# A graph attention and mixture-of-experts layer: accumulators kept in a 32-slot ring and stored once per node tile

## What is computed

```
h = einsum('nf,hfd->hnd', x, W);  a_s, a_d = h . att_src, h . att_dst       # per head
e = leaky_relu(a_s[:, src] + a_d[:, dst], 0.2)                              # edges and a self-loop of each node
for each head:
    m = segment_max(e, dst);  ex = exp(e - m[dst]);  den = segment_sum(ex, dst)
    out = segment_sum(h[src] * ex / den[dst], dst);  acc += softmax(gate)[head] * out
ln = layernorm(acc + bias + x);  result = ln @ Wo.T + bo
```

## Time and profile before

| | |
|---|---|
| median of 3 runs | 1814.36 us |
| lowest and highest | 1811.67, 1824.21 us |
| the profiled execution: time | 1812.91 us |
| its span | 1810.8 us |
| its mean granted TensorE clock | 0.824 of full speed |
| preparation | 0 to 190 us |
| edge phase: groups of products | 254 to 973 us |
| node stage, combine | 995 to 1118, 1118 to 1435 us |
| experts, final norm | 1450 to 1710, 1715 to 1808 us |
| PE, DVE, ACT, POOL busy, share of the span | 67, 58, 27, 37% |

### The profile page before, as it was taken

How to read it: one execution, slowest core, us unless ns; L and a number is a source line. 1 busy time by engine, 2 the same in 40 slices (tenths; PEclk the granted TensorE clock), 3 DMA queues, 4 the chain that set the end, 5 groups by cost and what they waited for, 6 DMA issues and landing times. The chain is left out here.

```text
span 1810.8 us, 29517 instructions
## 1 busy us (share of the span) xinstructions
PE 1220.3 (67%) x6148; PEld 994.7 (55%) x6149; DVE 1053.7 (58%) x3010; ACT 486.0 (27%) x1900; POOL 673.9 (37%) x781
## 2 busy tenths in 40 slices
PE   0795035666666776777784474999999179999800
PEld 0574023444444555555553353899998168999700
DVE  7656124556555666677785455678887433444357
ACT  0342011112221222222220233555553023333200
POOL 3000655656555454454300354244443201111164
PEclk9998556778887788897896656899999589999955
DMA  6015535566565656666644422334331395222155
GB/s 206 19 37 80 139 84 176 176 187 191 180 203 176 195 176 197 193 201 190 196 148 117 129 64 76 123 126 145 130 130 65 117 312 188 70 70 72 56 145 147
DMA packets 216712, 254.97 MB, mean 141 GB/s; under 512 B 53540, under 2 KB 190374, under 8 KB 212902
## 3 DMA queue, kind: packets, MB, share of 16 engines
q1 hardware_dynamic: 174262, 137.89, 24.9%
q0 software_dynamic: 30848, 103.40, 19.1%
q10 hardware_dynamic: 11504, 12.59, 2.1%
HBM read 138.88 MB, written 111.65 MB: 138 GB/s over the span
## 5 line engine op out<-in xcount | busy, mean ns | idle before, releaser
L683 POOL DMA_INDIRECT rows<-node_rows,srcT x391 | 381.7, 976 | 313.1 <-PE pO L947 179.7
L947 PE MATMUL pO<-rows,pw 128*128 x1184 | 381.1, 457 | 120.5 <-DVE pw L774 87.7
L790 DVE SCALAR_TENSOR_TENSOR acc<-acc,rsc,pO 128x257 f32<-128x257 f32 x592 | 282.4, 477 | 160.2 <-PE pO L947 74.0
L947 PEld LDWEIGHTS pO<-rows,pw 128*128 128x128 f32 x1184 | 243.0, 225 | 177.9 <-issue 143.2
L1355 PE MATMUL pW_<-W_again,aT 128*128 128x256 f32 x800 | 181.8, 381 | 0.0
L1355 PEld LDWEIGHTS pW_<-W_again,aT 128*128 128x128 f32 x800 | 148.9, 191 | 18.4
L1689 PEld LDWEIGHTS pHe<-xeT,w1e 128*128 128x128 f32 x1056 | 129.7, 194 | 9.9 <-DVE w1e L1727 6.6
L1689 PE MATMUL pHe<-xeT,w1e 128*128 128x128 f32 x1056 | 130.5, 277 | 5.7 <-DVE xeT L1707 4.8
L1745 POOL DMA_DIRECT2D ys_rows<-ye x66 | 35.7, 541 | 244.5 <-DVE ye L1737 244.5
L1698 PE MATMUL pYe<-w,hT 128*128 x528 | 125.3, 380 | 1.9 <-ACT hT L1668 1.1
L1668 ACT ACTIVATE hT<-pHe,b 128x128 f32<-128x128 f32 x264 | 75.5, 368 | 184.2 <-PE pHe L1689 172.7
(11 more groups left out here) (319 smaller groups left out, 2015.4 us busy)
## 6 DMA issues: line engine op xcount, KB each, us to landing
agg_rows<-acc SPq DMA_DIRECT2D x74, 1024.0 KB
w<-in_ffn_w SPq DMA_DIRECT2D x32, 512.0 KB, 5.6
xe<-xs_rows ACTq DMA_DIRECT2D x66, 128.0 KB, 2.0
ys_rows<-ye POOLq DMA_DIRECT2D x66, 128.0 KB, 2.0
rows<-node_rows,srcT POOLq DMA_INDIRECT x391
node_rows<-xna SPq DMA_DIRECT2D x25, 136.0 KB
xna<-in_x SPq DMA_DIRECT2D x5, 640.0 KB, 11.3
qs<-qT_y SPq DMA_DIRECT2D x25, 128.0 KB, 2.2
```

The lines of the kernel that those rows point to most:

```text
L683: pool.indirect_dma_start(rows[:, k % RING, :], None, node_rows[:, :], at_row(srcT[:, k:k + 1])).then_inc(s_rows[q % len(s_rows)], 16)
L790: dve.scalar_tensor_tensor(out=acc[:, k % V3, s % HG, 0:D + 1], in0=before, scalar=rsc[:, g % V2, s:s + 1], in1=pO[n % PB][:, 0:D + 1], op ...
L947: pe.matmul(pO[n % PB][:, 0:D + 1], pw[:, s // HG, s % HG, :], rows[:, ds(at[s % 4], 1), 0:D + 1].rearrange("p c f -> p (c f)"), start=Tru ...
```

## The change

Accumulators: `acc` becomes a ring of 32 slots, one per window (window number and 31). DVE loads the slots of four steps into registers and updates the slot in place. SP stores 8 slots, a node tile's 8 windows, once the tile's last step is accumulated (`end_at`, read into a register), waits until the store has landed, and raises `stored`; at each group's first step DVE loads from the table how far `stored` must be, and waits. 25 stores of 1.05 MB take the place of 74 of 1 MB. Since the divisor is the 257th column of what is stored, `dall`, `keep_den` and half of `md_rows` go. `topd` has four buffers, `flg` three; ACT, not SP, issues their transfers, and its list has another order. POOL reports a fetch one fetch later. Combine: SP loads the tile's rows of `AG` with a plain transfer, four buffers, `U` = 4; four small DVE operations per tile (`share`) form the factors `al`, and `own_rows` waits for them. The cleared accumulators are 128 x 8224 values, against 128 x 258.

```diff
-TAB = 20
+TAB = 36
+SLOTS_W, BATCH = 32, 8
-        agg_rows = dram("agg_rows", (GROUPS * G, P, D))
+        agg_rows = dram("agg_rows", (NT * BATCH, P, D + 1))
...
+                    line.do(dve.tensor_copy(win[:, 0, :], cs[:, 2, :]))
+                    line.do(dve.tensor_scalar(win[:, 0, :], win[:, 0, :], SLOTS_W - 1, None, ALU.bitwise_and))
+                    line.do(dve.tensor_scalar(win[:, 1, :], cs[:, 2, :], 2.0 - SLOTS_W, 1.0, ALU.add, ALU.max))
...
-            acc = sb("acc", [P, V3, HG, D + 2], ctx=ctx)
-            dall = sb("dall", [P, SP_], ctx=ctx)
+            acc = sb("acc", [P, SLOTS_W, D + 1], ctx=ctx)
...
-                        if q:
-                            landed(q - 1)
+                        if q > 1:
+                            landed(q - 2)
+                    landed(FETCHES - 2)
                     landed(FETCHES - 1)
...
-                    line.do(dve.memset(acc[:, V3 - 1, HG - 1, :], 0.0))
+                    line.do(dve.memset(acc[:, :, :], 0.0))
...
                     def accumulate(s):
                         def stage(g):
-                            k, n = 2 * g + s // HG, g * G + s
-                            if s % HG == 0 and k >= V3:
-                                dve.wait_ge(s_agg[k % V3], turns_of(k))
-                                wait(dve, den_in, k - V3)
+                            n = g * G + s
+                            if s == 0:
+                                upto_window = dve.value_load(step_tab[0:1, g, G + 1:G + 2], min_val=1, max_val=SP_)
+                                dve.wait_ge(stored, upto_window)
+                                dve.sem_inc(s_gate, 1)
+                                wait(dve, stat, g, KEEP)
+                            if s % 4 == 0:
+                                at[:] = nc.values_load_multi_w_load_instructions(step_tab[0:1, g, G + 4 + s:G + 8 + s], engines=(mybir.EngineType.DVE,), min_val=0, max_val=SLOTS_W - 1,
+                                                                                 skip_runtime_bounds_check_because="a window's slot")[1]
                             wait(dve, prod, g, s + 1)
                             if n:
                                 dve.wait_ge(acced.sem, n)
-                            if s == 0:
-                                wait(dve, stat, g, KEEP)
-                            before = acc[:, k % V3, s % HG - 1, 0:D + 1] if s % HG else acc[:, (k - 1) % V3, HG - 1, 0:D + 1]
-                            dve.scalar_tensor_tensor(out=acc[:, k % V3, s % HG, 0:D + 1], in0=before, scalar=rsc[:, g % V2, s:s + 1],
-                                                     in1=pO[n % PB][:, 0:D + 1], op0=ALU.mult, op1=ALU.add).then_inc(acced.sem, 1)
+                            mine = acc[:, ds(at[s % 4], 1), :].rearrange("p s f -> p (s f)")
+                            dve.scalar_tensor_tensor(out=mine, in0=mine, scalar=rsc[:, g % V2, s:s + 1], in1=pO[n % PB][:, 0:D + 1], op0=ALU.mult, op1=ALU.add).then_inc(acced.sem, 1)
...
-                    groups([(1, fifth), (1, last_flags), (1, last_max), (3, keep_den(0)), (3, keep_den(1)), (1, shrink), (1, exps), (0, copy_eq), (1, copy_top), (0, copy_as)])
+                    groups([(2, copy_top), (1, last_flags), (1, fifth), (1, last_max), (2, store_top), (0, load_flags), (1, shrink), (1, exps), (0, copy_eq), (0, copy_as)])
...
-                            sp.dma_start(agg_rows[k * HG:(k + 1) * HG, :, :].rearrange("s p f -> p s f"), acc[:, k % V3, :, 0:D]).then_inc(s_agg[k % V3], 16)
...
+                    sp.sem_inc(stored, 1)
+                    for b in range(NT):
+                        if b < NT - 1:
+                            steps = sp.value_load(end_at[0:1, b:b + 1], min_val=1, max_val=GROUPS * G)
+                            sp.wait_ge(acced.sem, steps)
+                            sp.sem_inc(s_gate, 1)
+                        else:
+                            wait(sp, acced, GROUPS - 1)
+                        s = b * BATCH % SLOTS_W
+                        sp.dma_start(agg_rows[b * BATCH:(b + 1) * BATCH, :, :].rearrange("w p f -> p w f"), acc[:, s:s + BATCH, :]).then_inc(s_agg, 16)
+                        if b < NT - 1:
+                            sp.wait_ge(s_agg, 16 * (b + 1))
+                            sp.sem_inc(stored, BATCH)
...
+                    def load(t, c, r):
+                        wait(sp, agg_in, t - U)
+                        sp.dma_start(AG[:, c, :, :].rearrange("p h f -> p (h f)"), row(agg_rows.rearrange("w (d h) f -> (w d) (h f)", h=H), t)).then_inc(s_AG[c], 16)
...
+                    pipeline(sp, NT, [(U + 6, store), (0, load)], U, 2)
...
                     def own_rows(t, c, r):
                         wait(act, agg_in, t - 2)
                         wait(act, aT_ps, t - 2)
+                        wait(act, al_in, t)
...
+                            if i == 0:
+                                dve.wait_ge(s_AG[c], (r + 1) * 16)
+                                wait(dve, own_in, t - 2)
+                                ins = dve.tensor_tensor(al[:, c % 2, 0, :], AG[:, c, :, D], share_of(2, t), ALU.mult)
```

More of the change, by code:

```diff
@@ L387, in _ @@
                     for j in range(2):
-                        mm = pe.matmul(pE[:, 448:448 + NT], same_win, by_tile[:, j, :], start=(j == 0), stop=(j == 1))
+                        mm = pe.matmul(pE[0:1, j * P:(j + 1) * P], cnt[:, j:j + 1], ident, start=True, stop=True)
                     mm.then_inc(steps_ps, 1)
@@ L637, in build @@
             consts.expect(5)
-            s_rows = [sem(f"s_rows{c}") for c in range(2)]
-            s_flg, s_top = [sem(f"s_flg{c}") for c in range(V2)], sem("s_top")
-            s_agg = [sem(f"s_agg{c}") for c in range(V3)]
+            s_rows = [sem(f"s_rows{c}") for c in range(3)]
+            s_flg, s_top = [sem(f"s_flg{c}") for c in range(V3)], [sem(f"s_top{c}") for c in range(V4)]
+            s_agg, stored = sem("s_agg"), sem("stored")
             fetched, as_in = sem("fetched"), Count(sem("as_in"))
@@ L812, in _ @@
                             line.do(ins)
-                    for i in (1, 0):
-                        wait(dve, md_ps, 2 - i)
-                        for j in range(2):
-                            n = slice(j * 4, min((j + 1) * 4, SJ))
-                            ins = dve.tensor_copy(mdT[:, n, :, i, :], banks[2 + 2 * i + j][:, 0:(n.stop - n.start) * P].rearrange("p (j d h) -> p j d h", d=DW, h=H))
-                        ins.then_inc(md_sb.sem, 1)
+                    wait(dve, md_ps, 1)
+                    for j in range(2):
+                        n = slice(j * 4, min((j + 1) * 4, SJ))
+                        ins = dve.tensor_copy(mdT[:, n, :], pO[2 + j][:, 0:(n.stop - n.start) * P].rearrange("p (j n) -> p j n", n=P))
+                    ins.then_inc(md_sb.sem, 1)
                 @block.scalar
@@ L958, in _ @@
                     mm.then_inc(md_ps.sem, 1)
-                    for i in (1, 0):
-                        wait(pe, md_sb, 1 - i) if i == 0 else wait(pe, den_in, 2 * GROUPS - 1)
-                        for j in range(SJ):
-                            mm = pe.transpose(banks[2 + 2 * i + j // 4][:, j % 4 * P:(j % 4 + 1) * P], (mall, dall)[i][:, j * P:(j + 1) * P], ident)
-                        mm.then_inc(md_ps.sem, 1)
+                    wait(pe, md_sb, 1)
+                    for j in range(SJ):
+                        mm = pe.transpose(pO[2 + j // 4][:, j % 4 * P:(j % 4 + 1) * P], mall[:, j * P:(j + 1) * P], ident)
+                    mm.then_inc(md_ps.sem, 1)
                 @block.sync
@@ L1296, in own_rows @@
                         wait(act, aT_ps, t - 2)
+                        wait(act, al_in, t)
                         act.sem_inc(s_gate, 1)
                         for h in range(H):
-                            ins = act.activation(own[:, c, h, :], tile(xna, t, 0, D), ACT.Copy, scale=al[:, 1, t, h:h + 1] if isinstance(t, int) else al[:, 1, ds(t, 1), h:h + 1].rearrange("p t h -> p (t h)"))
+                            ins = act.activation(own[:, c % 2, h, :], tile(xna, t, 0, D), ACT.Copy, scale=al[:, c % 2, 3, h:h + 1])
                         ins.then_inc(own_in.sem, 1)
@@ L1326, in keep_y @@
                         act.sem_inc(s_gate, 1)
-                        act.activation(tile(y_all, t, 0, D), yt[:, c, :], ACT.Copy).then_inc(y_kept.sem, 1)
+                        act.activation(tile(y_all, t, 0, D), yt[:, c % 2, :], ACT.Copy).then_inc(y_kept.sem, 1)
                     def keep_pick(t, c, r):
@@ L1387, in rank @@
                         wait(pe, placed, t - 1, 2)
-                        pe.matmul(pY[:, D + E:D + 2 * E], tri, both[:, c, :], start=True, stop=True)
-                        pe.matmul(pY[:, D + 2 * E:D + 3 * E], ones, both[:, c, :], start=True, stop=True).then_inc(rank_ps.sem, 1)
+                        pe.matmul(pY[:, D + E:D + 2 * E], tri, both[:, c % 2, :], start=True, stop=True)
```

(1 more changed line is left out.)

263 lines of the change are left out of this document (125 added, 138 removed).

## The result

The change takes 1843.8 us (median of 4 runs, 1832.8 to 1858.3), the kernel before 1819.3 (median of 4 runs); the ratio is 1.015, 95% interval 1.010 to 1.021. The forecast was 1773 and faster. The measured time lies inside the stated range (1712 to 1845), at its far end, but the direction was wrong: 24.5 us slower where 41.5 us faster was forecast. The profiled executions have spans of 1830.8 and 1810.8 us, so 20.0 us of the loss are in these two traces.

What follows compares the result with a forecast made beforehand. DVE was taken to bound an undisturbed group, PE a little behind. Products -45, start +2, preparation 0, tail -1.5, node stage -1, combine +4 gave -41.5 us: 1814.4 - 41.5 = 1773, range 1712 to 1845.

Steps and rivals of the forecast that it cites:

- What is left of the excess: Products: of 165 us over 37 groups like the last six, 52 stay, the rest absorbed as DVE trails PE.
- The 622: Products: 37 groups at 16.8 us each after the change, before adding what stays of the stalls.
- The base of 15.0 us for an undisturbed group: Products: the last six groups, 14.98 us each, taken as the length of all 37 when nothing disturbs them.
- The added 3.7 us on DVE: Each group: register loads, register steps and lost overlap add 3.7 us on DVE; bounds zero to 6.9.
- Step 0 (1.15): Group's first step: two register loads, arithmetic, register steps and events, some 1.15 us between spreads and first accumulate.
- The floor of the Trainium skill: Register loads on DVE: about 600 ns each by the page, 1.2 us more per group, some 45 us; not adopted.
- Start +2: Before the first group: clearing the larger ring takes 7 us more on DVE, mostly hidden; +2 of 0 to +7.
- Tail -1.5: Tail: the divisors' transposes and half the row table go, saving 1.5 us.
- Node stage -1: Node stage: five operations of 0.37 us fewer, partly hidden, saving 1 us.
- Combine +4: Start of the combine: own rows must wait for the divisor that comes with the tile, +4 us.
- it evens out: Rival for the products: 97 of the 165 us stay, 719 us, no change, 1813 to 1820; chance 0.23.
- slower: Rival: DVE's added time comes on top of the stalls; with 140 of 165 staying, 1861; over 1833; chance 0.19.

## Why the prediction was wrong

- **What is left of the excess (52 of 165 us): this step failed.** The products were forecast at 622 + 52 = 674 us and took 742.3, so 120 us stayed where 52 were forecast. The 622 was near: 37 groups as long as the last six take 37 x 16.63 = 615. Every term of the 52 came out higher: of the waits before an accumulate 30.5 us stayed (12 forecast), before rsc 33.6 (13), for pO 75.9 (15 and 31 that undisturbed groups have), before zT 37.6 (12). The argument was "DVE trails by four banks, so 2.8 us of each stall are free". The trace shows no such lead where it was needed: before an accumulate DVE has used up the finished products when five of the seven stalls begin, and before rsc the products that lie ready can't be taken, so a lead is of no use. The waits for pO say the same: 68.3 us before, 75.9 after, 67.8 even where no stall is; DVE waits for PE several times in each group. The sign that the prediction named for this, groups with gathers 3 us and more longer than those after them, is there: 20.7 against 16.6.
- **The base of 15.0 us for an undisturbed group.** It was read from the last six groups. The mean without stalls is 16.3 in one execution, so up to 50 of the 165 us of excess were no late release, and could not be won back by absorbing any: some 20 because the middle groups take 15.6 us, the rest in the first seven, where DVE waits for zT.
- **The added 3.7 us on DVE.** The bounds held, the parts were wrong. Step 0 (1.15) costs at most 0.15: its loads do take 1.1 us, but during the spreads. Loads in mid-group are 0.34 us as priced from PE's row, but 0 to 10 us in all by the runs that remove them, at most 0.3 per group, not the 1.0 and more of three loads. The register steps were put at 0.08 each; they cost 21 to 31 us in 592, 0.04 to 0.05 on average, and 0.10 at each accumulate that follows another. Without gathers the whole comes to 1.25 us per group, and with them to 0.7, where the prediction's net was 16.8 - 15.0 = 1.8.
- **The floor of the Trainium skill** ("DMA: Bandwidth & Descriptors", "Latency and other measured facts", about 600 ns for a `tensor_load`) is not seen on DVE either: 318 ns for one register, 343 for four.
- **The stores.** That their traffic is worth nothing by itself was right, and the runs without them agree, on chips without stalls. That DVE would not wait for `stored` was right too.
- **The smaller terms.** Start +2: measured +2.3, but +8.3 where the gathers do not hold the first group back; the memset had cover only from the stall. Tail -1.5: -1.0. Node stage -1: about -5 here, -2 on the second chip. Combine +4: +4.1 and +4.3, steady state 0: right on both.
- **The rivals.** The excess that stayed, 120 us by the prediction's own base (127 against the last groups as measured), lies between the 97 of "it evens out" and the 140 of "slower", nearer to the second, and 1843.8 is past the 1833 at which "slower" begins. The traces have the mechanisms of both: PE stops too when its banks are full, and a DVE with a longer chain catches nothing up. That the time still fell inside the range is luck as far as the forecast goes: the range reached up to 1845 because part of "slower" was in it.

What stays open is what makes the stalls. They appeared only in the traces of the result, with gathers in flight, in both kernels alike, and nothing tried on the four other chips brought them about.

## What to carry to other kernels

A wait that the engine's instruction used to carry itself is dearer when it stands at a register step ahead of it: here 0.1 us at each accumulate that follows the one it depends on, and slot addressing by registers cost 25 to 31 us where the traffic that it saved was worth nothing. Before removing traffic, look for a row in which someone waits for it; there was none. Slack argued from the number of buffers is worth something only if the trace shows that the buffers are full when the disturbance comes, and that nothing else stands ahead of them in the engine's order.

## What was not expected of the hardware

- The same kernel took 1819 us on the chip of the result and 1645 to 1651 on the four chips of the experiments. In the traces of the result DVE has waits that no instruction explains while gathers are in flight ("remote", 64 us in the products, 21.78 before the first group of the kernel before); the others have none. Of the 160 us between the two spans of the kernel before, 24 are the first group's start, 115 the products, and 15 the final norm, in which POOL gathers as well (98 us against 83). The products with `W`, with PE busy all the time, take the same 262 us on both.
- A register load on DVE takes 318 ns for one register and 343 for four, and runs while an earlier DVE instruction is still being computed, where that is long enough (loads at 967.53 and 968.30 under spreads from 967.70 to 970.05).
- Dependent accumulates of 0.48 us start 0.59 us apart when they carry the wait (ten of them in 5.79 us at the end of the kernel before), 0.69 to 0.70 when a register step of 57 ns carries it. The ten, in the trace of the kernel before taken again:

```profile
828.03 5.79 DVE L790 SCALAR_TENSOR_TENSOR acc<-acc,rsc,pO 128x257 f32<-128x257 f32 x10 [0.24 <-PE pO L947]
```
